# Attention front of a two-layer network: another order of the groups, modulation rows moved to the router, first loads in order of need

## The chip, the core and the metric

The kernel runs on one core of a Trainium2 chip. The metric is the device time of one execution in microseconds (us). A core has five engines that run side by side, each with its own instruction stream: TensorE (PE; PEld is its weight load), VectorE (DVE), ScalarE (ACT), GpSimd (POOL) and SyncE (SP), which here only issues DMA transfers. They wait for each other through semaphores.

## The reference, cut to what matters

Two layers; each is modulated attention, then a modulated mixture of experts. The change touches layer 0's attention and the router behind it.

```python
mod = (_silu(L0_c) @ L0_wmod).reshape(..., 6, 1, -1)      # rows sa, ca, ga, sb, cb, gb of 256
ga = (2 * (ga >= 0) - 1) * jnp.maximum(jnp.abs(ga), 0.25) # gb alike
h = _layernorm(x) * (1 + ca) + sa                          # x: 2048 x 256
q = (h @ Wq).reshape(.., 16, 16); k = h @ Wk; v = h @ Wv   # 16 heads, one key and value head of 16
scores = where(causal, q k / 4, -inf); out = softmax(scores) @ v
x = x + ga * (out @ Wo + bo)
h = _layernorm(x) * (1 + cb) + sb
x = x + gb * moe0(h)                                       # router: top 1 of 8, capacity 320
mod = (_silu(L1_c) @ L1_wmod)...                           # the same six rows for layer 1
```

## The kernel before

**Chunks, groups, units.** `phase_front` computes layer 0's attention. The 2048 queries are four chunks of 512 (`c`), the 16 heads four groups of 4 (`g`), so there are 16 groups `(c, g)`. A group of chunk `c` has `4(c+1)` units, one for each tile of 128 keys; in its last four, the diagonal units, only 4, 3, 2, 1 of the four query tiles are computed and POOL masks the diagonal block (L841). There are 160 units, numbered 0 to 159 in the order in which the groups run. A unit is 16 score matmuls in each of two halves (L424, four share the array at a time), two exponentials on ACT (L581, one for each half) and the value matmuls of the unit before (L440). So the two exponentials of unit n are number 2n+1 and 2n+2 of 320, and the first marks its start.

**Products for the maxima.** The softmax subtracts each row's maximum, so each group needs a first pass ahead of it: for 16 tiles of queries and each chunk of keys up to its own, four matmuls (L367) write a product to one of three PSUM banks (`f_r`, the ring), and DVE reduces it: 128x512 plainly (L641), the diagonal ones of 128, 256, 384 or 512 columns together with a causal mask (L638 and a read of its result). Below these are the full and the diagonal products. A group has 16, 32, 48 or 64 of them by chunk, 640 in all. When a group's last one is reduced, DVE makes its row of maxima (L645 to L649, `k_m2t`), SP writes it into the queries' tile (L749, 8 DMAs a group), and the group's first unit waits for it.

**The order of the work** is a table made by `front_schedule`. 45 products go in between the projections of chunks 2 and 3 (`EARLY`, `PRE`); the others are spread evenly over the units so that a group's last one comes 4 units (`MARGIN`) before its first unit, a unit taking at most 5 (`issued[u] = max(issued[u], issued[u + 1] - 5)`); what does not fit goes into unit 0. The ring also carries the rows of the modulation (M, L352: two fp32 matmuls, ACT copies them out, L534) and the output steps A, B, C of each tile of 128 tokens (A: turn the values, DVE divides, L390, L654, L655; B: turn back, ACT copies, L398, L538; C: output projection, DVE adds it to x and takes the statistics, L407, L661, L90). PE, DVE and ACT each take the entries in this one order.

**Queries through DRAM.** The projections make q and k as three bfloat16 parts (L328, L335, L529). SP writes the parts of a chunk to DRAM (L730) and reads them back in another layout (L740); a group's first product waits for that load (`q_in`). For chunk 0 the heads 4 to 15 have a load of their own (`q_rest`).

**Ahead and behind.** Before the projections DVE normalises x in four quarters (L78 to L83, L605), ACT issues the four loads of x, SP all others. Behind the front comes `phase_router` (layernorm, 8 logits, top 1, rank within the expert, then 16 scatters by POOL, L1274, `slots_ready` sets them free), then the experts. A phase starts when the one before has ended on all engines.

## Time and profile before

| | us |
|---|---|
| median of 3 runs | 1171.91 (1171.73 to 1172.45) |
| the profiled execution | 1172.97 |
| its span in the trace | 1171.3 |
| PE, DVE, ACT, POOL busy over the span | 84%, 54%, 46%, 25% |
| unit 0 starts, unit 159's exponentials end | 83.45, 517.3 |
| first router instruction | 529.9 |

The profile's page gives the busy time of each engine and, in 40 slices of 29.3 us, its busy tenths. PEclk is the clock that TensorE was granted, 1.00 being 2.4 GHz and 0.50 being 1.2 GHz. A row of windows gives each engine's busy time and its number of instructions (x) in a stretch; a row of the timeline gives the start, the length, engine, line, what was written from what, and in brackets how long the engine had been idle and what ended that.

### The profile page before, as it was taken

Reading aid. Unit: us, or ns where it says so; the run is one execution under the profiler, and the core shown is the slowest. Engines: PE = TensorE matmul, PEld = TensorE weight load, DVE = VectorE, ACT = ScalarE, POOL = GpSimd, SP = SyncE. Lnnn points to the kernel's source line nnn. Section 1 sums busy time; section 2 is a strip of 40 time slices with the busy share of each in tenths; the row PEclk is TensorE's granted clock in tenths of the full one; section 3 lists DMA queues with packets and bytes.
Section 4 is the critical chain, followed back from the end, with each engine's and each line's share of the span. In section 5 each row is a group of like instructions: output and inputs, shape, how many; then the busy total and the mean of one; then the engine's idle time right before and its main releaser. Section 6 shows DMA issues by size and latency. Waiting matters only on the chain. (4 is left out here: it accounts for less than half of the span.)

```text
span 1171.3 us, 25113 instructions
## 1 busy us (share of the span) xinstructions
PE 985.8 (84%) x9938; PEld 639.1 (55%) x9943; DVE 629.3 (54%) x1719; ACT 535.6 (46%) x834; POOL 297.4 (25%) x344
## 2 busy tenths in 40 slices
PE   4888999999999999985079999649557599999994
PEld 2434444344334544332057777537335599999993
DVE  4256889999999999345100000185676633333331
ACT  1543665666666777764023222155045443333330
POOL 3001431101001100110502222235720035455442
PEclk9988999999999999998579999969789799999997
DMA  6682000100003000008314555210045722322333
GB/s 205 165 156 41 3 2 3 69 28 2 3 3 3 3 2 3 1 1 292 119 28 115 168 115 168 37 54 1 1 162 186 235 41 47 49 45 49 48 47 90
DMA packets 73406, 81.66 MB, mean 70 GB/s; under 512 B 23121, under 2 KB 64465, under 8 KB 72609
## 3 DMA queue, kind: packets, MB, share of 16 engines
q1 hardware_dynamic: 58912, 61.18, 18.7%
q0 software_dynamic: 12288, 17.10, 8.7%
q10 hardware_dynamic: 2112, 2.10, 0.6%
q8 instruction: 64, 1.05, 0.4%
q14 instruction: 30, 0.24, 0.1%
HBM read 58.19 MB, written 24.13 MB: 70 GB/s over the span
## 5 line engine op out<-in xcount | busy, mean ns | idle before, releaser
L581 ACT ACTIVATE k_prob<-f_s 128x1024 f32<-128x1024 f32 (+3 forms) x320 | 270.1, 896 | 123.2 <-PE f_s L424 122.2
L641 DVE TENSOR_REDUCE k_mpart<-f_r 128x1 f32<-128x512 f32 x384 | 250.0, 684 | 12.4 <-PE f_r L367 10.3
L367 PE MATMUL f_r<-k_ks,k_qs 112*32 112x512 bf16 (+3 forms) x2560 | 213.2, 354 | 11.8 <-DVE k_mpart L641 6.6
L424 PE MATMUL f_s<-k_qs,k_ks 114*32 114x512 bf16 (+3 forms) x2560 | 176.6, 351 | 6.4 <-DMA k_qs<-k_m2t 4.2
L440 PE MATMUL f_o<-k_prob,k_vaug 128*32 128x512 f32 (+3 forms) x1280 | 150.4, 532 | 0.5 <-POOL k_prob L841 0.3
L841 POOL TENSOR_SCALAR_AFFINE_SELECT k_prob<-k_prob 128x256 f32<-128x256 f32 x128 | 51.4, 406 | 384.5 <-ACT k_prob L581 383.2
L367 PEld LDWEIGHTS f_r<-k_ks,k_qs 112*32 112x32 bf16 x2560 | 70.8, 95 | 138.3 <-DVE k_mpart L641 64.8
L638 DVE CUSTOM_DVE_ANT_0 k_unread<-f_r,k_causal 128x128 bf16<-128x128 f32 (+3 forms) x256 | 120.6, 484 | 31.6 <-PE f_r L367 30.7
L424 PEld LDWEIGHTS f_s<-k_qs,k_ks 114*32 114x32 bf16 x2560 | 65.5, 97 | 75.0 <-issue 21.4
L1975 DVE TENSOR_TENSOR mid<-silu_g,e_u 128x512 f32<-128x512 f32 x39 | 26.8, 688 | 126.7 <-PE e_u L1880 126.7
L1415 DVE SCALAR_TENSOR_TENSOR outr<-p_o,rows,k_mod 128x256 f32<-128x256 f32 x16 | 7.7, 484 | 141.3 <-PE p_o L1372 141.3
L1880 PEld LDWEIGHTS e_g<-xT,wg 128*128 128x128 f32 x624 | 76.9, 195 | 3.3 <-ACT xT L1935 1.4
L1880 PE MATMUL e_g<-xT,wg 128*128 128x128 f32 x624 | 77.5, 278 | 0.9 <-ACT xT L1935 0.9
L1361 PE MATMUL p_h<-rowsT,k_wi 128*128 128x320 f32 x256 | 73.3, 446 | 4.9 <-issue 3.8
L1880 PE MATMUL e_u<-xT,wu 128*128 128x128 f32 x624 | 76.4, 276 | 0.0
L2023 POOL DMA_INDIRECT xb<-h_rows,k_tok_of x39 | 45.0, 1155 | 121.3 <-PE e_x L1874 66.1
L2032 POOL DMA_INDIRECT sum<-y,k_row_of x39 | 62.0, 1591 | 53.0 <-DVE y L1986 50.2
L1401 ACT ACTIVATE mid<-p_h 128x320 f32<-128x320 f32 x64 | 28.0, 437 | 103.2 <-PE p_h L1361 103.2
L1891 PE MATMUL e_y<-k_w1T,mid 128*128 x312 | 73.6, 379 | 0.0
L1880 PEld LDWEIGHTS e_u<-xT,wu 128*128 128x128 f32 x624 | 73.2, 193 | 0.0
L1361 PEld LDWEIGHTS p_h<-rowsT,k_wi 128*128 128x128 f32 x256 | 49.4, 195 | 26.6 <-issue 8.2
L1891 PEld LDWEIGHTS e_y<-k_w1T,mid 128*128 128x128 f32 x312 | 56.3, 190 | 6.1
(299 smaller groups left out, 1280.3 us busy)
## 6 DMA issues: line engine op xcount, KB each, us to landing
r_raw<-in_L_ffn_w_dram SPq DMA_DIRECT2D x24, 512.0 KB, 5.8
k_wi<-in_L_ffn_wi_dram SPq DMA_DIRECT2D x8, 1024.0 KB, 5.1
k_wo_e<-in_L_ffn_wo_dram SPq DMA_DIRECT2D x8, 1024.0 KB, 7.7
k_qs<-q_dram SPq DMA_DIRECT2D x6, 768.0 KB, 9.6
sum<-k_x SPq DMA_DIRECT2D x8, 512.0 KB, 7.0
q_dram<-k_q_parts SPq DMA_DIRECT2D x12, 256.0 KB, 6.4
disp<-k_wmod SPq DMA_DIRECT2D x2, 1310.0 KB, 7.2
rows<-disp SPq DMA_DIRECT2D x8, 262.0 KB, 2.7
```

What stands on the lines that cost most here:

```text
L367: last = nc.tensor.matmul(dst[32 * j:32 * (j + 1), :], qs[0:KROWS, c, GH * g + hs, q0:q0 + 32], ks[0:KROWS, QC * ck:QC * ck + w], start=Tr ...
L424: last = nc.tensor.matmul(sc[h % 2][32 * j:32 * (j + 1), i, off:QC], ks[0:KALL, k0:k0 + 32], qs[0:KALL, c, GH * g + 2 * pair + i, off:QC], ...
L440: last = nc.tensor.matmul(ot[32 * j:32 * (j + 1), off:QC], vaug[:, kt, :], prob[:, u % 2, j, off:QC], start=(kt == 0), stop=(kt == TQ * (c ...
L581: nc.scalar.activation(prob[:, u % 2, 2 * pair:2 * pair + 2, off:QC], sc[h % 2][:, :, off:QC], ACT.Exp, scale=HD ** -0.5).then_inc(e_done, 1)
L638: nc.vector.tensor_tensor_reduce(unread[:, r % RING, 0:w], bank(r)[:, 0:w], causal[:, QC - w:QC], 1.0, NEG, ALU.add, ALU.max, mpart[:, s % ...
L641: nc.vector.reduce_max(mpart[:, s % 2, hs, t, ck:ck + 1], bank(r)[:, 0:w], AX.X).then_inc(ring_used[r % RING], 1)
L841: nc.gpsimd.affine_select(out=block_, in_=block_, compare_op=ALU.is_ge, fill=0.0, base=0, pattern=[[0, 2], [1, P]], channel_multiplier=-1) ...
L1361: last = nc.tensor.matmul(ph[n % 2][:, :], wi[:, s, t, P * n:P * (n + 1)], rowsT[:, s, t, :], start=(t == 0), stop=(t == KH - 1))
L1880: last = nc.tensor.matmul(out[:, P * c:P * (c + 1)], w[:, s, F1 * t + P * c:F1 * t + P * (c + 1)], xT[:, s, t, :], start=(t == 0), stop=(t ...
L1891: last = nc.tensor.matmul(py[s][:, :], m[:, s, P * c:P * (c + 1)], k.w1T[:, e, 2, D * c:D * (c + 1)], start=(c == 0), stop=(c == FT - 1))
L2023: nc.gpsimd.indirect_dma_start(out=xb[:, s, :], out_offset=None, in_=k.h_rows, in_offset=bass.IndirectOffsetOnAxis(ap=k.tok_of[:, b:b + 1] ...
L2032: nc.gpsimd.indirect_dma_start(out=k.sum1, out_offset=bass.IndirectOffsetOnAxis(ap=k.row_of[:, b:b + 1], axis=0), in_=y[:, s, :], in_offse ...
```

## The change

It has four parts. (1) `ORDER`: the groups run as (0,0), (1,0), (2,0), (3,0), then (3,1) to (3,3), (2,1) to (2,3), (1,1) to (1,3), (0,1) to (0,3). The 45 early products are then 16 of chunk 0 and 29 of chunk 1. The output steps of a chunk follow its last group, so those of chunk 0 come last. All four chunks' outputs need a place (`oT`, `kept`), and POOL's steps (gate, bias, clearing, `rstd2`) are put at other units. (2) The ring keeps only the modulation rows GA, SB, CB, GB of layer 0. The unused rows SA and CA are dropped; the six of layer 1 are computed in layer 0's router from a load of their own, with 6 fp32 matmuls of 512 columns, 3 copies and 5 DVE instructions. (3) The first loads go out in the order in which they are used; three quarters of x move from ACT's to SP's queue. (4) The row of maxima takes 4 DMAs a group, each of two rows, for 8.

```diff
-MOD_ORDER = [GA, SA, CA, SB, CB, GB] + list(range(MODS, 2 * MODS))
+MOD_ORDER = [GA, SB, CB, GB]
-ORDER = [(c, g) for c in range(NC) for g in range(NG)]
+ORDER = ([(c, 0) for c in range(NC)] + [(NC - 1, g) for g in range(1, NG)]
+         + [(c, g) for c in range(NC - 2, -1, -1) for g in range(1, NG)])
...
-            first = (start[4] + 2, start[8] + 2, start[15] - 4, NU)[c]
+            first = min(start[s] + TQ * (c + 1) + 2, NU - len(order) + 1) if c else NU
...
-    NROWDMA = 8
+    NROWDMA = 4
...
-        oT = sb("oT", [P, 2, NG, QC])
+        own = sb("oT", [P, 2, NG, QC])
+        oT = [own[:, 0], own[:, 1], kept[:, 0], kept[:, 1]]
...
-            for c in range(NC):
-                act.dma_start(quarter(k.x, c), xv[:, TQ * c:TQ * (c + 1), :]).then_inc(x_in[c], 16)
+            act.dma_start(quarter(k.x, 0), xv[:, 0:TQ, :]).then_inc(x_in[0], 16)
...
                 if u == NU - 6:
-                    scale_row(0, CB)
-                    gate_row(0, GB)
-                if u == NU - 4:
-                    for m in (CA, CB):
-                        scale_row(1, m)
-                    for m in (GA, GB):
-                        gate_row(1, m)
+                    scale_row(CB)
+                    gate_row(GB)
...
                 for b in range(4):
-                    for part in range(2):
-                        dst = qs[BROW + part:BROW + part + 1, c, GH * g:GH * (g + 1), :]\
-                            .rearrange("o h (t b r) -> o (h t) b r", b=4, r=32)[:, :, b, :]
-                        sp.dma_start(dst, m2t[32 * b + NT * part:32 * b + NT * (part + 1), s, :]).then_inc(rows_in[s], 16)
+                    dst = qs[BROW:BROW + 2, c, GH * g:GH * (g + 1), :].rearrange("o h (t b r) -> o (h t) b r", b=4, r=32)[:, :, b, :]
+                    sp.dma_start(dst, m2t[32 * b:32 * (b + 1), s, :]).then_inc(rows_in[s], 16)
...
-                if u == 16:
+                if u == 12:
                     fold_gate()
-                if u in (17, 18, 19, 24):
-                    add_bias((17, 18, 19, 24).index(u))
-                if u == 26:
+                if u in range(13, 17):
+                    add_bias(u - 13)
+                if u == 24:
                     clear()
...
             if layer == 0:
+                sp.dma_start(wmod[:, :, :], a.L1_wmod.rearrange("(t p) n -> p t n", p=P)).then_inc(wmod_in, 16)
                 xv = k.sum0[0:T, :].rearrange("(i p) d -> p i d", p=P)
...
+            if layer == 0:
+                pe.wait_ge(wmod_in, 16)
+                pe.wait_ge(hT_ready, 2 * NC)
+                for n in range(3):
+                    for t in range(KH):
+                        last = nc.tensor.matmul(tp[n // 2][n % 2][:, :], k.mod[:, 1, GB, P * t:P * (t + 1)], wmod[:, t, QC * n:QC * (n + 1)],
+                                                start=(t == 0), stop=(t == KH - 1))
+                    last.then_inc(rows_done, 1)
+
             pe.wait_ge(chosen_ready, 1)
...
                 nc.vector.tensor_copy(scat[:, 0, :], small[3][:, :]).then_inc(slots_ready, 1)
+                dve.wait_ge(mod_ready, 3)
+                m = k.mod[:, 1, :, :].rearrange("p (b m) d -> p b m d", b=2)
...
```

**The first loads, on SP.** `k_x` is x, `k_wq`, `k_wk`, `k_wv` are the projections' weights, `k_wmod` the modulation's. Before:

```order
L714 DMA k_c_col<-in_L_c_dram 128x2x1 x2
L717 DMA k_wmod<-in_L_wmod_dram 128x2x512
L719 DMA k_wq<-in_L_attn_Wq_dram 128x2x256
L719 DMA k_wk<-in_L_attn_Wk_dram 128x2x16
L719 DMA k_wv<-in_L_attn_Wv_dram 128x2x16
L720 DMA k_kpart<-in_kpart_dram 128x4
L721 DMA k_bo<-in_L_attn_bo_dram 128x256
L722 DMA k_wo<-in_L_attn_Wo_dram 128x2x256
L724 DMA k_wmod<-in_L_wmod_dram 128x2x1024
L725 DMA k_wmod<-in_L_wmod_dram 128x2x1536
```

And of the change:

```order
L711 DMA k_wmod<-in_L_wmod_dram 128x2x512
L713 DMA k_wq<-in_L_attn_Wq_dram 128x2x256
L713 DMA k_wk<-in_L_attn_Wk_dram 128x2x16
L713 DMA k_wv<-in_L_attn_Wv_dram 128x2x16
L714 DMA k_kpart<-in_kpart_dram 128x4
L715 DMA k_bo<-in_L_attn_bo_dram 128x256
L717 DMA k_x<-in_L_attn_x_dram 128x4x256 x3
L718 DMA k_wmod<-in_L_wmod_dram 128x2x1024
L719 DMA k_wo<-in_L_attn_Wo_dram 128x2x256
```

The quarters 1 to 3 of x now stand behind the weights in the same queue, and layer 1's modulation weights (128x2x1536) are no longer loaded here.

**The last products between the projections of chunk 2, on PE.** L335 takes a part away, L343 is the values' projection of chunk 2, L328 the first projection of chunk 3. Before:

```order
L335 MATMUL f_o<-k_ks,k_minus 128x512
L367 MATMUL f_r<-k_ks,k_qs 32x128 x4
L367 MATMUL f_r<-k_ks,k_qs 32x256 x4
L343 MATMUL f_r<-k_wv,k_h 128x16 x8
L328 MATMUL f_s<-k_h,k_wq_by_d 128x512 x2
```

And of the change:

```order
L339 MATMUL f_o<-k_ks,k_minus 128x512
L370 MATMUL f_r<-k_ks,k_qs 32x512 x4
L370 MATMUL f_r<-k_ks,k_qs 32x128 x4
L347 MATMUL f_r<-k_wv,k_h 128x16 x8
L332 MATMUL f_s<-k_h,k_wq_by_d 128x512 x2
```

The two products were of group (0,1) and are now of (1,0), whose queries are chunk 1's.

**The first units, on PE.** L424 (L427) are scores, L440 (L443) values, L352 (L355) a modulation row. Before, from unit 0 into unit 2:

```order
L424 MATMUL f_s<-k_qs,k_ks 32x512 x16
L424 MATMUL f_s<-k_qs,k_ks 32x384 x8
L367 MATMUL f_r<-k_ks,k_qs 32x256 x4
L424 MATMUL f_s<-k_qs,k_ks 32x384 x8
L440 MATMUL f_o<-k_prob,k_vaug 32x512 x4
L352 MATMUL f_r<-k_wmod,k_silu_c 128x256 x2
L424 MATMUL f_s<-k_qs,k_ks 32x256 x8
```

And of the change, the whole of unit 0 and the start of unit 1:

```order
L427 MATMUL f_s<-k_qs,k_ks 32x512 x8
L370 MATMUL f_r<-k_ks,k_qs 32x384 x4
L427 MATMUL f_s<-k_qs,k_ks 32x512 x8
L370 MATMUL f_r<-k_ks,k_qs 32x512 x16
L370 MATMUL f_r<-k_ks,k_qs 32x128 x4
L370 MATMUL f_r<-k_ks,k_qs 32x512 x8
L370 MATMUL f_r<-k_ks,k_qs 32x256 x4
L370 MATMUL f_r<-k_ks,k_qs 32x512 x8
L370 MATMUL f_r<-k_ks,k_qs 32x384 x4
L370 MATMUL f_r<-k_ks,k_qs 32x512 x20
L370 MATMUL f_r<-k_ks,k_qs 32x128 x4
L370 MATMUL f_r<-k_ks,k_qs 32x512 x8
```

Unit 0 had no product and has 20 now.

## Rows read from the trace of the kernel before

**Rows 1.** The page's 40 slices: busy tenths of PE, and TensorE's clock.
```profile
PE   4888999999999999985079999649557599999994
...
PEclk9988999999999999998579999969789799999997
```

In rows 2 each row is: stretch, its length, busy us (x instructions) of PE, PEld, DVE, ACT, POOL, then PEclk, the share of the DMA engines and GB/s.

**Rows 2.** Windows cut where units 0, 4, 8, 12, 28, 44, 68, 76, 92, 140, 144, 152, 156 start.
```profile
83.40:99.85 16.45, 11.99 (x153) 5.23 (x148) 5.70 (x26) 6.35 (x11) 3.21 (x8) 0.83 0.68 114
99.85:115.40 15.55, 15.10 (x196) 7.57 (x190) 11.19 (x41) 7.25 (x13) 3.20 (x8) 0.85 0.02 3
115.40:129.95 14.55, 13.67 (x200) 6.88 (x196) 11.86 (x35) 7.09 (x13) 3.20 (x8) 1.00 0.01 1
129.95:173.70 43.75, 42.93 (x684) 19.99 (x680) 39.02 (x115) 29.04 (x41) 20.11 (x24) 1.00 0.02 3
173.70:220.60 46.90, 43.56 (x716) 18.35 (x708) 45.07 (x126) 27.04 (x34) 7.44 (x17) 1.00 0.02 3
220.60:287.95 67.35, 65.83 (x1007) 29.27 (x1001) 62.47 (x159) 43.76 (x54) 7.42 (x17) 1.00 0.11 42
287.95:306.95 19.00, 18.64 (x328) 7.88 (x324) 18.26 (x48) 13.34 (x17) 3.21 (x8) 1.00 0.02 3
306.95:352.75 45.80, 43.89 (x712) 16.87 (x705) 44.99 (x106) 29.04 (x33) 3.23 (x8) 1.00 0.01 3
352.75:472.40 119.65, 118.40 (x1924) 55.77 (x1920) 113.94 (x254) 86.69 (x99) 9.61 (x24) 1.00 0.11 3
472.40:481.85 9.45, 7.96 (x114) 3.43 (x110) 3.11 (x12) 5.49 (x9) 3.20 (x8) 1.00 0.02 3
481.85:502.90 21.05, 20.58 (x222) 7.98 (x218) 3.74 (x10) 16.70 (x20) 0.00 (x0) 1.00 0.01 2
502.90:510.95 8.05, 7.48 (x100) 2.13 (x96) 5.99 (x21) 7.54 (x8) 1.01 (x1) 1.00 0.00 1
510.95:517.45 6.50, 5.66 (x96) 1.89 (x88) 0.00 (x0) 5.21 (x8) 3.23 (x8) 1.00 0.01 3
```

**Rows 3.** The start, DVE's first instruction and the first loads' times to landing.
```profile
13.02 0.29 DVE L677 COPY k_wk_rep<-k_wk 128x256 f32<-128x256 f32 x1 [13.02 <-DMA k_wv<-in_L_attn_Wv_dram]
...
k_x<-in_L_attn_x_dram ACTq DMA_DIRECT2D x4, 512.0 KB, 7.6
k_wmod<-in_L_wmod_dram SPq DMA_DIRECT2D x1, 1536.0 KB, 12.8
```

**Rows 4.** Window in the start (columns as in rows 2; the last is GB/s).
```profile
6.00:8.00 2.00, 0.00 (x0) 0.00 (x0) 0.00 (x0) 0.59 (x1) 0.00 (x0) 1.00 1.07 379
```

**Rows 5.** Source line L740, 50 to 52 us: the load of chunk 1's queries.
```profile
L740 SPq DMA_DIRECT2D k_qs<-q_dram x3: 319/422/423, 50.6 to 51.4; - x3
...
DMA to landing us min/median/max: 7.6/11.4/13.2
```

**Rows 6.** Timeline: chunk 2's values' projection, diagonal and full reductions, an output's addition.
```profile
60.72 1.96 PE L343 MATMUL f_r<-k_wv,k_h 128*128 128x16 f32 x16 [0.32 <-DVE k_mpart L638]
...
71.28 0.29 DVE L638 CUSTOM_DVE_ANT_0 k_unread<-f_r,k_causal 128x128 bf16<-128x128 f32 x1 [0.94 <-PE f_r L367]
...
72.93 0.29 DVE L638 CUSTOM_DVE_ANT_0 k_unread<-f_r,k_causal 128x128 bf16<-128x128 f32 x1
...
470.03 1.94 DVE L641 TENSOR_REDUCE k_mpart<-f_r 128x1 f32<-128x512 f32 x3
...
522.14 0.42 DVE L661 TENSOR_TENSOR k_x<-k_x,f_r 128x256 f32<-128x256 f32 x1 [0.46 <-PE f_r L407]
```

**Rows 7.** Timeline: PE at unit 4.
```profile
98.76 1.04 PE L424 MATMUL f_s<-k_qs,k_ks 114*32 114x512 bf16 x8 [2.85 <-DMA k_qs<-k_m2t]
```

**Rows 8.** Timeline: two fp32 matmuls of 512 columns; in the router the ranks, the first scatter.
```profile
27.35 1.88 PE L328 MATMUL f_o<-k_h,k_wk_rep 128*128 128x512 f32 x4
...
557.06 0.29 PE L1052 MATMUL r_prank<-r_chosen_bf,k_before 128*128 128x128 bf16 x1 [4.72 <-DVE r_chosen_bf L1143]
...
564.28 1.23 POOL L1274 DMA_INDIRECT disp<-r_hx,r_scat  x1 [33.67 <-DVE r_scat L1177]
```

More of the change, by code:

```diff
@@ L274, in phase_front @@
         ZW = E * CAP // P * DW // 2
-        zeros = wmod[:, 1, :, :].rearrange("p t n -> p (t n)")[:, 0:ZW]
+        zeros = room[:, 0:ZW]
         marks = sb("marks", [P, 3, E * CAP // P], U32)
         x_in = [sem(f"f_x_in{c}") for c in range(NC)]
-        c_in, wmod_in = sem("f_c_in"), [sem(f"f_wmod_in{n}") for n in range(3)]
+        c_in, wmod_in = sem("f_c_in"), [sem(f"f_wmod_in{n}") for n in range(2)]
         wq_in, const_in, wo_in = sem("f_wq_in"), sem("f_const_in"), sem("f_wo_in")
@@ L450, in _ @@
                         last = nc.tensor.matmul(ot[:, 2 * m + half:2 * m + half + 1],
-                                                wmod[:, 0, t, D * m + P * half:D * m + P * (half + 1)],
-                                                silu_c[:, 0, t, 0:1], start=(t == 0), stop=(t == KH - 1))
+                                                wmod[:, t, D * m + P * half:D * m + P * (half + 1)],
+                                                silu_c[:, t, 0:1], start=(t == 0), stop=(t == KH - 1))
             last.then_inc(col_done, 1)
@@ L625, in gate_row, with scale_row @@
                 step(nc.vector.scalar_tensor_tensor(gate, gate_sgn[:, :], -1.0, gate_mag[:, :], ALU.add, ALU.mult))
-            def scale_row(layer, m):
-                have(layer, m)
-                step(nc.vector.tensor_scalar_add(k.mod[:, layer, m, :], k.mod[:, layer, m, :], 1.0))
+            def scale_row(m):
+                have(m)
+                step(nc.vector.tensor_scalar_add(k.mod[:, 0, m, :], k.mod[:, 0, m, :], 1.0))
             def maxima(r, n):
@@ L721, in _ @@
             sp.dma_start(bo[:, :], a.L0_attn_bo.partition_broadcast(P)).then_inc(const_in, 16)
+            for c in range(1, NC):
+                sp.dma_start(quarter(k.x, c), xv[:, TQ * c:TQ * (c + 1), :]).then_inc(x_in[c], 16)
+            sp.dma_start(wmod[:, :, 2 * D:MODS * D], wm[:, :, 2 * D:MODS * D]).then_inc(wmod_in[1], 16)
             sp.dma_start(wo[:, :, :], a.L0_attn_Wo.rearrange("(t p) n -> p t n", p=P)).then_inc(wo_in, 16)
-            sp.dma_start(wmod[:, 0, :, 512:MODS * D], wm[0][:, :, 512:MODS * D]).then_inc(wmod_in[1], 16)
-            sp.dma_start(wmod[:, 1, :, :], wm[1]).then_inc(wmod_in[2], 16)
             def spill(c):
@@ L808, in clear @@
             def clear():
-                pool.wait_ge(ring_done, at[("M", MOD_ORDER[-1])] + 1)
+                for part in range(3):
+                    pool.wait_ge(spilled[part], 16 * NC)
                 nc.gpsimd.memset(zeros[:, :], 0.0).then_inc(zero_set, 1)
@@ L842, in _ @@
                                                 pattern=[[0, 2], [1, P]], channel_multiplier=-1).then_inc(masked, 1)
-            ln_rstd(nc, pool, k, NC - 1, var2_ready, rstd2_ready)
+            for n in range(len(rstd_after), NC):
+                rstd2(n)
             pool.wait_ge(rstd2_ready, NC)
@@ L1106, in _ @@
                 nc.scalar.activation(ex[j][:, :, :], tmp[j][:, :, :], ACT.Exp).then_inc(exp_done, 1)
+            if layer == 0:
+                for n in range(3):
+                    act.wait_ge(rows_done, n + 1)
+                    nc.scalar.copy(k.mod[:, 1, 2 * n:2 * n + 2, :].rearrange("p m d -> p (m d)"),
+                                   tp[n // 2][n % 2][:, :]).then_inc(mod_ready, 1)
             if layer == 1:
```

70 lines of the change are left out of this document (41 added, 29 removed).

## The prediction

> **What bounds the kernel now.** I read the page's slices first [rows 1]. TensorE is busy in nine tenths or more of nearly every slice from 120 to 470 us and its clock stands at 2.4 GHz there; the front is the longest piece, and the change touches it and the router only. So the question is what a unit costs, and I cut the front where its units start [rows 2]. The reader is to see three regimes.
> - In the 48 units 92 to 139 the windows hold 119.65 us, 2.49 us a unit, with PE busy for 118.40 and DVE for 113.94. Four products a unit load both engines fully.
> - In units 28 to 43 (five products each) DVE is busy 45.07 of 46.90 us and PE 43.56: DVE ends last, 2.93 a unit.
> - Units 152 to 155 have no product and take 8.05 us, 2.01 each, with ACT busy 7.54 and DVE waiting or on small rows. The exponentials end last there.
>
> So a product near the end is nearly missing work, and at the start it is dear. Units 0 to 11 are worse than any: 46.55 us for 12 small diagonal units [rows 2], PE busy 11.99 of the first 16.45. Unit 4's scores waited 2.85 us for the row of maxima [rows 7]. SP had issued it behind the loads of chunk 3's queries. The clock is 0.83 and 0.85 in the first two rows, and eleven modulation rows go through the ring here.
>
> **The units, part by part.** The order tables of both kernels were laid beside each other, unit by unit. 104 of the new kernel's units have the same shape, the same products and the same output steps as units of the old one, only elsewhere: its 4 to 19 are the old 76 to 91 (45.80 us), 20 to 67 the old 92 to 139 (119.65), 84 to 107 the old 44 to 67 (67.35), 120 to 135 the old 12 to 27 (43.75); one modulation row moves between them. I price them at what they took, 276.55 together [rows 2], and no gain or loss is in them. The other 56 old units took the rest of 434.05 us: 46.55 (0 to 11), 46.90 (28 to 43), 19.00 (68 to 75), and 9.45 + 21.05 + 8.05 + 6.50 = 45.05 (140 to 159), together 157.5. The 56 new ones hold the same 163 products, in other company:
> - Units 0 to 3 have 35 products, 20 of them in unit 0. DVE: 23 full ones at 1.94/3 = 0.647, 12 diagonal ones at (72.93 - 71.28)/4 = 0.41 [rows 6], 0.8 for a row of maxima: 20.6. PE needs less. I take 23, because I expect some low clock behind unit 0. Ends 20.6 and 30.
> - 68 to 83: three products. A full unit sheds one (512 columns at 2.4 GHz, 0.21) and comes from 2.49 to about 2.29, the four diagonal ones 7.0 in all: 34.5. Ends: 31 (as with no product, 2.01) and 40 (as with four).
> - 108 to 119: 2.67 products: 24, ends 22 and 29.
> - 136 to 143: two small products, two output steps C, and POOL's `rstd2` ahead of a mask at unit 138: 17, ends 14.5 and 20.
> - 144 to 151: eight diagonal units with four small products each. DVE 16 x 0.41 + 0.8 per four, with the output steps: 16, ends 14 and 18.
> - 152 to 159: eight diagonal units with no product and eight output steps. Units 156 to 159 took 6.50 with none and 140 to 143 9.45 with four and a wait of about 1.3 for their row of maxima [rows 2]: 2 x 8.1 = 16.2. Ends 13 and 20.
>
> Sum 130.7, so the units give back 157.5 - 130.7 = 26.8 us. Eight modulation rows fewer on the ring are a part of it, the rest is waiting that is now filled. The row of maxima with 4 DMAs instead of 8 is priced at nothing: four units pass between its last product and its use, and where they are full units that covers it.
>
> The burst in unit 0 is the place where another rule speaks. The trace has TensorE pausing for DVE again and again through units 28 to 43, 3.34 us in 46.90, at a clock of 1.00; it has the clock at 0.83 where PE was busy 11.99 of 16.45 [rows 2]. The Trainium skill, page "TensorE: Matmul & The Clock Gate", section "A second HAM failure mode: psum-queue depth-cycling", says that matmuls which cycle through PSUM banks with small pauses can make the clock swing between its two levels. By that rule the heavy units would not hold 2.4 GHz and the sum would be the last rival's below; the trace agrees for long pauses and not for short ones.
>
> **The start.** DVE's first instruction waits for the values' weights until 13.02 [rows 3]; everything up to unit 0 follows from there. They share the DMA engines with four quarters of x (512 KB each) and two larger loads of modulation weights, of which the first steps need one quarter only. What they need is 512 (x) + 512 (modulation) + 256 (query weights) + 32 KB = 1.31 MB. At 340 to 379 GB/s, the rate of the windows at 6 us [rows 4], that is 3.6 us of transfer; it starts near 3.4 and small rows come last, so I take 8.3 us, a gain of 4.7 (ends 3.5 and 6). The second quarter of x, 0.5 MB more, is there about 1 us later, before DVE has done the first.
>
> **A wait that is added.** The last two products between chunk 2's projections are now of group (1,0) and wait for chunk 1's queries. That load is issued until 51.4 and its last part lands 13.2 later, at 64.6 [rows 5]. PE reaches this place at 60.3, just before the values' projection at 60.72 [rows 6]. Both shift with the start, so PE stands 4.3 us, and behind it stand the values' projection and all of chunk 3's. Ends: 0 (if the load is quicker with less traffic) and 5. This eats the gain of the start.
>
> **Chunk 3's projections.** 27 products are reduced between them, now half of them full: 0.24 more for each of 9 in the stretch where DVE sets the pace, less a row of maxima (0.8) that moves into unit 0: + 1.5. Ends 0 and 3.
>
> **The tail.** One more output step C stands behind unit 159. It runs while ACT copies the last values; its DVE work (0.42 for the addition [rows 6], as much for the statistics) delays the first division a little: + 0.7. Ends 0 and 1.5.
>
> **The router.** PE ends its logits 4.72 us before it gets the chosen experts at 557.06 [rows 8]. Two fp32 matmuls of 512 columns take 1.88 [rows 8], so the six new ones take 5.6, 0.9 too long; DVE, which needs the ranks, has steps of its own for most of that: + 0.5 (ends 0 and 2). DVE's five instructions stand behind the slots, beside the scatters that begin at 564.28 [rows 8]. Layer 1's load of 1536 KB goes ahead of the copies of x and of the experts' weights; at the rate of the start it takes 4.2 us of the DMA engines, which were quiet before the scatter. I price it at nothing; if it delays the scatter, 4.
>
> **Sum.** - 26.8 - 4.7 + 4.3 + 1.5 + 0.7 + 0.5 = - 24.5 against the profiled execution's 1172.97: 1148.5. That execution lies 1.06 above the median of 1171.91, so the median to expect is **1147.4**. Its own range, the ends not all on one side at once: 1140 to 1155.
>
> **Rivals.**
> - *The wait isn't there.* Less traffic ahead of the queries, 0 instead of 4.3: 1143. For it: 2.5 MB fewer in the first 20 us. Against: those had landed by 20.3 (7.5 + 12.8 [rows 3]), 30 us before the load in question.
> - *A unit with fewer products costs no less.* If units 68 to 83, 108 to 119 and 136 to 143 cost what units with four products cost, 40 + 29 + 18.5 instead of 75.5: + 12, 1159. For it: no unit of before has three. Against: units 152 to 155 at 2.01.
> - *Small diagonal units are slow in themselves.* 12 new units of chunk 0 stand at the end. At the 46.55 of units 0 to 11 instead of about 24.4: + 22, 1170. For it: the chain of exponential, mask and values is the same. Against: units 156 to 159 take 6.50 for four, and unit 4 was held by a DMA [rows 7].
> - *Slower: the clock.* Unit 0 leaves PE idle for more than half of some 12 us. If the clock then stays at 1.2 GHz while PE feeds DVE, a unit of five products needs 2 x (2.49 + 0.21) us of PE where DVE needs 2.93, 2.5 more each. Over units 1 to 16 that is 40: 1187. It decides from about 10 units on. Against: in the second row of [rows 2] PE was busy 15.10 of 15.55, and the clock was back at 1.00 afterwards.
> - That the change doesn't do what it says is excluded by its order table.
>
> **Chances.** Forecast 0.62, no wait 0.12, fewer products no cheaper 0.13, diagonal units slow 0.07, clock 0.06. The range for 8 in 10 goes from 1138 (no wait, and some ends low) to 1161. A change under 0.2% (2.3 us) can't be told from none: faster 0.92, within 0.03, slower 0.05.
>
> **What the profile after would show.** DVE's first instruction near 8.3; PE idle some 4 us before the values' projection of chunk 2, released by a DMA; unit 0 starting at 83.45 - 4.7 + 4.3 + 1.5 = 84.6 and lasting some 12 us with DVE full; units 20 to 67 in 119.7 us; unit 159 done near 492; the router some 24 us earlier and of equal length. The prediction is wrong if the clock stays at 0.5 beyond unit 4, if the same-shaped stretches take other times, or if the last twelve units need more than 3 us each.

## The result: less than half of the forecast gain

The changed kernel took 1162.09 us (median of 6, 1161.18 to 1164.53) beside 1172.24 for the kernel before on the same chip: ratio 0.9909, interval 0.9893 to 0.9925. It is faster, but the forecast was 1147.4 with a range from 1138 to 1161, so the time lies outside. Between the profiled executions the gain is 1172.97 - 1162.2 = 10.8 us where 24.5 were forecast; 13.7 are missing. The kernel before took 1170.79 to 1173.49 us (medians) in the sessions of the experiments, so kernels of different sessions are compared by their ratios and not by their medians.

The page's slices of the kernel after, which answer to [rows 1] (busy tenths of PE, and TensorE's granted clock):

```profile
PE   5889899999999999957099999558657599999994
...
PEclk9987999999999999998599999769788799999998
```

The front is still the longest piece, and from 145 to 493 us PE is busy for nine tenths or more of every slice. The windows cut at the new kernel's units show more. They answer to [rows 2]: length, then busy us of PE, PEld, DVE, ACT, POOL, then PEclk, DMA share and GB/s. The rows are, in order, chunk 3's projections, then units 0 to 3, 4 to 19, 20 to 67, 68 to 83, 108 to 119, 120 to 135, 136 to 143, 144 to 151 and 152 to 159.

```profile
61.70:87.20 25.50, 23.24 (x173) 11.36 (x175) 15.27 (x45) 7.12 (x10) 0.00 (x0) 0.83 0.61 122
...
87.20:112.85 25.65, 23.52 (x249) 8.69 (x244) 20.06 (x51) 6.45 (x11) 3.21 (x8) 0.67 0.32 57
...
112.85:161.35 48.50, 44.95 (x716) 17.43 (x712) 46.38 (x109) 29.89 (x35) 14.69 (x15) 1.00 0.01 2
161.35:280.05 118.70, 117.47 (x1928) 54.07 (x1924) 113.93 (x254) 86.68 (x99) 11.84 (x25) 1.00 0.01 3
280.05:315.05 35.00, 34.87 (x583) 14.97 (x578) 28.52 (x71) 28.84 (x33) 3.21 (x8) 1.00 0.01 3
...
381.30:405.95 24.65, 24.52 (x424) 10.51 (x420) 18.42 (x55) 21.05 (x25) 3.21 (x8) 1.00 0.01 3
405.95:448.95 43.00, 42.17 (x680) 19.43 (x676) 39.17 (x117) 28.18 (x38) 6.41 (x16) 1.00 0.01 3
448.95:467.55 18.60, 16.75 (x268) 7.42 (x264) 10.50 (x48) 13.36 (x17) 4.08 (x9) 1.00 0.56 4
467.55:486.40 18.85, 17.02 (x338) 8.24 (x338) 16.17 (x75) 11.14 (x18) 6.41 (x16) 1.00 0.02 4
486.40:503.55 17.15, 15.89 (x219) 7.17 (x211) 5.91 (x18) 12.11 (x21) 6.41 (x16) 1.00 0.01 3
```

Against the forecast, stretch by stretch (us):

| stretch | forecast | measured | difference |
|---|---|---|---|
| start of unit 0 | 84.6 | 87.25 | + 2.65 |
| units 0 to 3 | 23 | 25.65 | + 2.65 |
| units 4 to 19 | 45.80 | 48.50 | + 2.70 |
| units 20 to 67 | 119.65 | 118.70 | - 0.95 |
| units 68 to 135 | 169.6 | 168.9 | - 0.7 |
| units 136 to 143 | 17 | 18.60 | + 1.60 |
| units 144 to 151 | 16 | 18.85 | + 2.85 |
| units 152 to 159 | 16.2 | 17.15 | + 0.95 |
| first expert's first product less the end of the units | 78.45 | 78.05 | - 0.4 |
| from there to the end | 576.6 | 578.8 | + 2.2 |

Lines 5 and 9 are worked out: 34.5 + 67.35 + 24 + 43.75 against 448.95 - 280.05; 594.71 - 517.45 + 1.2 against 581.60 - 503.55. The end of the units is the end of the last value matmul here (503.55), and 517.45 lies in the last value matmuls, which end at 517.68. The table of times ahead of the prediction has 517.3 for the end of unit 159's exponentials; in the trace the last one ends at 516.73. The units took 416.35 us where 407.25 were forecast and 434.05 were taken before.

The timeline of the kernel after on DVE and PE, answering to [rows 3] and [rows 6] (start, us, engine, line, operation, and in brackets the idle time before and what ended it):

```profile
8.53 0.29 DVE L675 COPY k_wk_rep<-k_wk 128x256 f32<-128x256 f32 x1 [8.53 <-DMA k_wv<-in_L_attn_Wv_dram]
...
11.95 1.40 DVE L78 BATCH_NORM_STATS2 k_stats<-k_x 128x6 f32<-128x256 f32 x4 [1.20 <-DMA k_x<-in_L_attn_x_dram]
```

```profile
61.07 0.73 PE L370 MATMUL f_r<-k_ks,k_qs 112*32 112x512 bf16 x8 [4.54 <-DMA k_qs<-q_dram]
61.73 3.60 PE L347 MATMUL f_r<-k_wv,k_h 128*128 128x16 f32 x16
...
457.89 0.64 PE L443 MATMUL f_o<-k_prob,k_vaug 128*32 128x256 f32 x8 [1.22 <-POOL k_prob L841]
```

The first row is the forecast gain of the start (8.3 was said). The second is a wait that was said not to be: the second quarter of x isn't there in time. The third is the added wait, 4.54 us for 4.3. Right behind it the values' projection takes 3.60 us where it took 1.96 before [rows 6]: the granted clock stands at 0.5 from 59.9 to 70.2 us, and again from 87.2 to 104.3. In the kernel before it was at 0.5 for 3.4 us four times and for 6.8 once in the whole front.

### The profile page after: what moved, and what is told of

The parts are those of the page before. It is cut to its first block and busy times, and to the rows that moved or that the text cites. A ratio compares the mean times of both kernels' runs of the same rounds, so it can differ in the third digit from the quotient of the medians.

```text
span 1160.4 us, 24988 instructions
## 1 busy us (share of the span) xinstructions
PE 980.0 (84%) x9918; PEld 635.9 (55%) x9923; DVE 632.0 (54%) x1714; ACT 534.2 (46%) x830; POOL 297.8 (26%) x344
## 5 line engine op out<-in xcount | busy, mean ns | idle before, releaser
L370 PE MATMUL f_r<-k_ks,k_qs 112*32 112x512 bf16 (+3 forms) x2560 | 212.0, 359 | 16.2 <-DVE k_mpart L639 7.3
L427 PE MATMUL f_s<-k_qs,k_ks 114*32 114x512 bf16 (+3 forms) x2560 | 173.9, 350 | 1.9 <-ACT k_prob L579 1.3
L443 PE MATMUL f_o<-k_prob,k_vaug 128*32 128x512 f32 (+3 forms) x1280 | 146.5, 531 | 1.5 <-POOL k_prob L841 1.4
L427 PEld LDWEIGHTS f_s<-k_qs,k_ks 114*32 114x32 bf16 x2560 | 64.2, 97 | 79.3 <-issue 27.8
L2002 DVE TENSOR_TENSOR mid<-silu_g,e_u 128x512 f32<-128x512 f32 x39 | 26.8, 688 | 124.7 <-PE e_u L1907 124.7
L2050 POOL DMA_INDIRECT xb<-h_rows,k_tok_of x39 | 45.3, 1161 | 121.5 <-PE e_x L1901 64.5
```

Source lines behind the costliest of these rows:

```text
L370: last = nc.tensor.matmul(dst[32 * j:32 * (j + 1), :], qs[0:KROWS, c, GH * g + hs, q0:q0 + 32], ks[0:KROWS, QC * ck:QC * ck + w], start=Tr ...
L427: last = nc.tensor.matmul(sc[h % 2][32 * j:32 * (j + 1), i, off:QC], ks[0:KALL, k0:k0 + 32], qs[0:KALL, c, GH * g + 2 * pair + i, off:QC], ...
L443: last = nc.tensor.matmul(ot[32 * j:32 * (j + 1), off:QC], vaug[:, kt, :], prob[:, u % 2, j, off:QC], start=(kt == 0), stop=(kt == TQ * (c ...
L2050: nc.gpsimd.indirect_dma_start(out=xb[:, s, :], out_offset=None, in_=k.h_rows, in_offset=bass.IndirectOffsetOnAxis(ap=k.tok_of[:, b:b + 1] ...
```

## The experiments

Each was timed in several executions beside the kernel before, except one that ran once. Ratios are to the kernel before, with their interval.

**The change without its order.**

```diff
-ORDER = ([(c, 0) for c in range(NC)] + [(NC - 1, g) for g in range(1, NG)] + ...)
+ORDER = [(c, g) for c in range(NC) for g in range(NG)]
```

> Everything of the change but the order of groups: the groups run in the old order (and the output steps start at their old units), first loads, router rows and the four row DMAs stay new. Theory A (the new order pays about 11 us: units 0 to 159 went from 434.05 to 416.3 us, of which some 3 are the eight modulation rows that left the ring, and it costs the 4.54 us wait for chunk 1's queries): this kernel keeps the start (PE's first turn 3.3 us early), has no such wait, and keeps the 2 us lost behind the router: about 1169 us, units 0 to 159 in some 431 us. Theory B (the order pays little, the start and the router's rows carry the change): 1164 us or less, and the units in under 427. In both, if the 0.24 us that PE loses between two experts comes from the code around it and not from the order, it is here too.

1163.71 us, 0.9922 (0.9900 to 0.9945). That overlaps the change's interval: the new order, on which nearly the whole forecast rested, is worth about nothing in this kernel. Its windows (units 0 to 3, 4 to 11, 12 to 19, 20 to 159):

```profile
80.10:93.40 13.30, 11.90 (x156) 5.09 (x152) 5.71 (x27) 6.34 (x12) 3.20 (x8) 0.85 0.76 140
93.40:116.90 23.50, 19.72 (x360) 9.03 (x356) 21.41 (x71) 11.93 (x20) 7.89 (x19) 1.00 0.01 2
116.90:138.45 21.55, 18.81 (x336) 9.03 (x332) 19.42 (x59) 14.00 (x18) 13.04 (x13) 1.00 0.01 3
138.45:503.60 365.15, 354.12 (x5516) 154.78 (x5512) 315.04 (x781) 249.61 (x303) 43.77 (x100) 1.00 0.05 10
```

All 160 units take 423.5 us: 10.55 of the 17.7 us that the units gained come with the old order kept. Units 0 to 11 lost 9.75 of their 46.55 [rows 2]. Of the 10.55, 1.0 is no part of the change: units 100 to 103 took 11.11 us in the profiled execution of the kernel before and 10.07 to 10.10 in the next experiment's kernel and here, because PE's value matmuls paused once in unit 100. Its cause stayed open. The order brings the other 7.15, and it costs as much ahead of them: unit 0 starts at 80.1 here and at 87.25 in the change. Theory B came true, with 1163.71 for "1164 or less" and 423.5 for "under 427".

**One part alone in the kernel before: rows of maxima with 4 DMAs.**

```diff
-                    for part in range(2):
-                        dst = qs[BROW + part:BROW + part + 1, ...]
-                        sp.dma_start(dst, m2t[32 * b + NT * part:32 * b + NT * (part + 1), s, :])
+                    dst = qs[BROW:BROW + 2, ...]
+                    sp.dma_start(dst, m2t[32 * b:32 * (b + 1), s, :])
```

> The kernel before with one part of the change alone: a row of maxima is brought back with 4 DMAs instead of 8. Theory A (PE's wait of 2.85 us at unit 4 and that of some 1.4 us at unit 140 are the 8 DMAs' issuing and landing): the two waits shrink to under 0.5 us each, units 4 to 7 take 12.5 to 13.5 instead of 15.55, units 140 to 143 take 8.1 instead of 9.46; the kernel about 1169 us. Theory B (the row waits behind the loads of chunk 3's queries, and the old output steps hold units 140 to 143): both waits stay over half their length, 1171 to 1173 us.

1169.21 us, 0.9977 (0.9963 to 0.9992). Windows of units 0 to 3, 4 to 7 and 140 to 143:

```profile
85.70:99.35 13.65, 12.46 (x153) 5.36 (x149) 5.69 (x26) 6.35 (x11) 3.22 (x8) 0.81 0.54 98
99.35:113.00 13.65, 12.96 (x196) 6.75 (x192) 11.16 (x41) 7.21 (x13) 3.22 (x8) 1.00 0.02 3
468.90:476.95 8.05, 7.89 (x118) 3.47 (x112) 2.92 (x12) 5.49 (x10) 3.22 (x8) 1.00 0.02 3
```

They took 16.45, 15.55 and 9.45 [rows 2], and unit 4's scores wait no longer [rows 7]. Theory A for the waits: both were the 8 DMAs. The wait of 2.85 us ended at 98.76, before unit 4's first exponential at 99.85, so it is units 0 to 3 that are 2.8 shorter; with the 1.4 of units 140 to 143 the DMAs cost 4.2. The 1.9 of units 4 to 7, where the theory looked for the wait, go with TensorE's clock, which was 0.85 there and is 1.00. The median moved by 2.0 only, and in the profiled execution unit 0 started 2.3 us later than before.

**The change without its second part: the second layer's rows back in the front.**

```diff
-MOD_ORDER = [GA, SB, CB, GB]
+MOD_ORDER = [GA, SA, CA, SB, CB, GB] + list(range(MODS, 2 * MODS))
```

> The whole change but its second part: the second layer's modulation rows and the two rows that moved with them stay in the front (twelve rows less two, in units 1 to 12), its weights are loaded behind the first loads; order, first loads and 4 DMAs are new. Theory A (the eight rows cost the old front some 8 of the 10.4 us that the change gained there with the old order kept, because each holds PE for 1.13 us at the place where DVE and PE are both full): here they cost as much, units 0 to 19 take 80 us or more instead of 74.1, the router and the experts give 1.5 to 2 us back: about 1167 to 1169 us. Theory B (in the new order PE waits for DVE in units 0 to 19, so the rows hide): units 0 to 19 under 76 us, and the kernel 1161 to 1163 us. The 0.24 us lost between two experts should be gone if it comes with the router's rows.

1166.32 us, 0.9958 (0.9942 to 0.9975). Windows of units 0 to 3, 4 to 11 and 12 to 19, and the first expert's first product:

```profile
86.60:112.20 25.60, 23.47 (x248) 8.65 (x244) 20.06 (x51) 6.44 (x11) 3.21 (x8) 0.67 0.32 57
112.20:143.50 31.30, 29.45 (x392) 13.87 (x388) 24.99 (x60) 16.34 (x26) 5.37 (x12) 1.00 0.01 2
143.50:167.30 23.80, 23.36 (x364) 9.44 (x360) 22.42 (x49) 16.36 (x18) 6.92 (x3) 1.00 0.01 1
```

```profile
587.47 3.03 PE L1369 MATMUL p_h<-rowsT,k_wi 128*128 128x320 f32 x5 [1.03 <-ACT rowsT L1406]
```

Units 0 to 19 take 80.7 us, 6.55 more than the change's 74.15: 0.82 us for each of eight rows (POOL's bias additions also stand at their old units here). That price isn't the same everywhere: with the old order the units of the two kernels with 4 DMAs, rows in the front and rows in the router, differ by 3.1 us in all. The expectation says twelve rows less two; the kernel has all twelve. Behind the units the router with its rows costs nothing: from unit 159's exponential to the first expert 78.7 us before, 78.7 in the kernel with the old order and router rows, 80.1 here without router rows and 80.3 in the change. The 1.5 us come with the order (one more output step behind the units), not with the rows. The table shows less of it because it counts from the last value matmul, and in the new order that one stands behind an output step.

**Gate row, bias and modulation rows later.**

```diff
-GATE_AT = 8
+GATE_AT = 72
-        extras[1 + n].append(("M", m))
+        extras[67 + n].append(("M", m))
-                if u == 12:            # fold_gate
+                if u == 74:
-                if u in range(13, 17): # add_bias
+                if u in range(75, 79):
```

> Gate row, folding of the gate and the bias additions move from units 8 to 16 to units 72 to 78, where DVE has three products a unit, and the four modulation rows from units 1 to 4 to 67 to 70. Theory A (units 4 to 19 took 48.47 us and not the 45.80 of the same units of before because the four gate instructions of DVE, 1.53 us, and POOL's bias additions stand in units that DVE bounds): units 4 to 19 come back to 45.8 to 46.3, units 68 to 83 stay within 0.5 us of 35.0, units 0 to 3 lose the modulation rows' 0.5 us or so; the kernel takes 1158.5 to 1160 us. Theory B (units 4 to 19 are slow because DVE starts them late behind the burst of unit 0): they stay within 0.7 us of 48.47 and the kernel takes 1161.5 to 1162.5 us.

1163.16 us, 0.9915 (0.9892 to 0.9937): no gain. Windows of units 0 to 3, 4 to 19, 20 to 67 and 68 to 83:

```profile
87.40:109.80 22.40, 20.29 (x236) 6.72 (x232) 19.31 (x51) 5.50 (x8) 3.25 (x8) 0.62 0.36 64
109.80:155.65 45.85, 43.54 (x712) 16.70 (x708) 45.14 (x106) 29.52 (x34) 3.23 (x8) 1.00 0.01 2
155.65:275.65 120.00, 118.78 (x1932) 58.32 (x1928) 114.88 (x259) 87.06 (x100) 11.84 (x25) 1.00 0.01 3
275.65:314.90 39.25, 38.13 (x596) 18.09 (x592) 29.18 (x70) 29.99 (x36) 14.76 (x15) 1.00 0.01 3
```

Here the two forecasts that failed come true: 22.40 for 23, and 45.85 for 45.80. So the 5.3 us missing in units 0 to 19 are the four modulation rows and the gate's work, which the comparison of shapes had left out. Units 0 to 3 lost 3.25 us, where 0.5 had been expected of their rows. Half of theory A fell, though: units 68 to 83 did not hide it, they took 4.25 more and units 20 to 67 1.3 more. There PE is full (34.87 of 35.00), and a row or a step that leaves DVE's tight place enters PE's.

**Six products ahead instead of five.**

```diff
-        issued[u] = max(issued[u], issued[u + 1] - 5)
+        issued[u] = max(issued[u], issued[u + 1] - 6)
```

> Of the plan one number: a unit may hold 6 products ahead of its need instead of 5, so that unit 0 has 9 products and not 20, and units 1 to 7 have 6 each; the 19 units of the front take the same products. Theory A (units 0 to 3 and the begin of unit 4 were slow because PE paused for DVE through the burst in unit 0 and the clock stood at 0.5 from 87.2 to 104.3 us): with fewer products at one place the clock stays at 1.00 for most of it, units 0 to 19 take 70 to 72 us together instead of 74.1, the kernel 1158 to 1160 us. Theory B (DVE does the same products in the same time, wherever they stand, and the clock falls for the same pauses, only spread): units 0 to 19 within 1 us of 74.1, the kernel 1161.5 to 1163 us.

1161.28 us, 0.9913 (0.9895 to 0.9931). Units 0 to 19:

```profile
86.60:160.50 73.90, 66.46 (x956) 25.60 (x952) 66.23 (x159) 36.37 (x46) 17.96 (x23) 0.93 0.11 21
```

Theory B: 73.9 us for 74.15, although the clock stood at 0.5 for 10 us in three pieces and not for 17. That doesn't show that the low clock is free, because the products stand elsewhere too, and PE was busy as long as DVE (66.46 and 66.23). A cleaner pair is the change and the kernel with fewer narrow products below, which has the same instructions up to unit 135. Its clock came back at 101.3 us and not at 104.3; its units 0 to 3:

```profile
87.50:111.55 24.05, 21.93 (x248) 8.38 (x244) 20.05 (x51) 6.35 (x12) 3.20 (x8) 0.72 0.34 60
```

That is 1.6 us less than the change's 25.65. Unit 0, the burst, took 12.5 and 12.7 us, at the low clock in both; unit 1 took 4.28 and 5.75, and its value matmuls 1.03 and 1.93. So in the burst the low clock cost nothing that these traces show, and in unit 1 it cost 1.5 us.

**No product between chunk 2's last step and chunk 3's projections.**

```diff
-EARLY = {2: (2,) * 9, 3: (3,) * 9}
+EARLY = {2: (2,) * 8 + (0,), 3: (0, 0, 0, 5, 5, 5, 5, 5, 4)}
```

> The last product between chunk 2's projections and all between chunk 3's three projections are moved behind these, so that PE has 6 fp32 products of chunk 3 to do while chunk 1's queries land; the number of early products stays 45. Theory A (the wait of 4.54 us costs its length, and 1.3 more because the clock stands at 0.5 from 59.9 to 70.2 us behind it): the wait is gone, the clock stays at 1.00 there, unit 0 starts 4 to 6 us earlier (81 to 83 instead of 87.25) and the kernel takes 1156.5 to 1158 us. Theory B (DVE sets the pace between chunk 3's projections, 27 products, and they can't start before the queries are there): the wait only moves, unit 0 starts less than 2 us earlier and the kernel takes 1160.5 or more.

1157.97 us, 0.9870 (0.9839 to 0.9901), from executions in two groups, three at 1155.0 and three at 1160.9 to 1163.3. The profiled one is of the upper group. Its window from the values' projection to unit 0:

```profile
61.30:85.40 24.10, 21.80 (x161) 9.18 (x163) 14.86 (x44) 7.03 (x11) 0.00 (x0) 0.79 0.82 161
```

The wait is gone, but the clock fell at 75.4 for 27.3 us, and unit 0 started only 1.85 us earlier, at 85.4. Neither theory is settled by it; the next one was made for that.

**Chunk 1's queries in two loads.**

```diff
-                load_queries(c, 0, H, q_in[c])
+                load_queries(c, 0, GH if c == 1 else H, q_in[c])
+                if c == 1:
+                    load_queries(c, GH, H, q_rest[1])
```

> Of the load of chunk 1's queries the first four heads (a quarter of its 768 KB) are brought in first with a semaphore of their own, as chunk 0's are; the products of (1,0) need no more. Nothing else is moved. Theory A (PE's 4.54 us wait before chunk 2's values is the landing of 768 KB, and the low clock from 59.9 to 70.2 us follows from it): the wait falls to under 1 us, unit 0 starts 4 to 6 us earlier (81.5 to 83), the kernel 1156 to 1158.5 us. Theory B (the load is late by its issue and its way, not by its size): the wait stays over 3 us, 1161 to 1162.5 us. Theory C (the wait goes, but the clock falls later in the front all the same): unit 0 at 82 to 84, the kernel 1158.5 to 1160.5 us.

1155.04 us, 0.9862 (0.9837 to 0.9887). PE at the place of the wait, and the window from there to unit 0:

```profile
58.48 0.46 PE L370 MATMUL f_r<-k_ks,k_qs 112*32 112x512 bf16 x8
59.26 1.96 PE L347 MATMUL f_r<-k_wv,k_h 128*128 128x16 f32 x16 [0.33 <-DVE k_mpart L636]
```

```profile
59.30:82.95 23.65, 21.97 (x170) 9.63 (x174) 15.88 (x49) 7.19 (x11) 0.00 (x0) 0.90 0.72 147
```

Theory A: the wait was the landing of 768 KB of which 192 were needed. No wait is left, and the values take 1.96 us again. Unit 0 starts 4.3 us earlier, at 82.95: PE had no wait of 4.54 and took 1.8 less from the values to unit 0, but reached this place 2.0 later than in the change (its clock had stood at 0.5 for 6.8 us before, and for 3.4 there). By the ratios the kernel gains 5.5 us, and the two intervals leave 2 to 9, so the median can't tell the gain from the wait's length. With this the order is worth something: 0.9862 against 0.9922 with the old order, which has no such wait (its last products between chunk 2's projections are of chunk 0): 7 us.

**The second quarter of x first.**

```diff
+            sp.dma_start(quarter(k.x, 1), xv[:, TQ:2 * TQ, :]).then_inc(x_in[1], 16)
             sp.dma_start(kpart[:, :], a.kpart).then_inc(const_in, 16)
```

> One load is moved: the second quarter of x goes ahead of the constants and the bias (behind the values' weights) on SP's queue. Theory A (DVE waits 1.20 us for it before its second statistics, and PE's first turn hangs on that): the wait shrinks to 0 to 0.5, PE's first turn starts about 1 us earlier than 15.41, and all of that reaches the end: about 1161.1 us. Theory B (the DMA engines are full there, so that an earlier quarter holds up the first quarter and the weights by as much, or ACT and POOL wait for the constants instead): first turn within 0.3 us, 1162 us.

1161.93 us, 0.9905 (0.9882 to 0.9928). DVE's second statistics:

```profile
10.50 1.40 DVE L78 BATCH_NORM_STATS2 k_stats<-k_x 128x6 f32<-128x256 f32 x4
```

They start at 10.50 without a wait and PE's first turn at 14.06 instead of 15.41. Unit 0 gains 0.8, because the wait for the queries grew to 4.93. Theory A for the place; at the end it can't be told from nothing.

**Two groups of chunk 1 at the begin.**

```diff
+ORDER = ([(0, 0), (1, 0), (1, 1), (2, 0)] + [(NC - 1, g) for g in range(NG)]
+         + [(c, g) for c in range(NC - 2, -1, -1) for g in range(1 + (c == 1), NG)])
```

> The order begins with two groups of chunk 1 ((0,0), (1,0), (1,1), (2,0), (3,0)), the rest as in the change; unit 0 has 13 products and the next ones 5, and 8 units fewer stand at the end. Theory A (the lump of products that the new order owes before unit 12 is what makes the begin dear): units 0 to 11 and what they hold come cheaper by 3 us or more, the last 24 units the same, the kernel 1158 to 1160 us. Theory B (what is missing at the begin comes back at the end and the other way round, since PE and DVE are both near full over the whole front): 1161 to 1163.5 us. The wait for chunk 1's queries (4.54 us) is in this one too.

1155.87 us, 0.9869 (0.9847 to 0.9891), better than either theory. Units 0 to 11, 12 to 19 and 20 to 67:

```profile
86.65:131.30 44.65, 39.93 (x572) 16.61 (x568) 38.33 (x107) 20.20 (x30) 8.04 (x19) 0.89 0.19 34
131.30:154.20 22.90, 20.99 (x360) 8.05 (x352) 22.48 (x55) 13.54 (x17) 14.82 (x14) 1.00 0.01 3
154.20:276.30 122.10, 119.89 (x1960) 56.09 (x1956) 117.83 (x264) 87.16 (x100) 10.26 (x25) 1.00 0.01 2
```

Units 0 to 11 take 44.65 us instead of 51.15, with 8 products fewer and DVE busy for 38.33 us instead of 43.74; units 20 to 67 give 3.4 us back, and units 136 to 159 take 3.1 more, where theory A had them unchanged. All units together: 3.6 less. The profiled execution is 6.3 shorter; 2.3 of that lie behind the first expert, where the code is the same.

**Fewer narrow products at the end (run once).** Three of four heads' maxima of the last three groups are left out, so those groups' values are others.

```diff
-        rows = [(hs, qt) for hs in range(GH) for ...]
+        rows = [(hs, qt) for hs in range(GH - 1 if s > 12 else 0, GH) for ...]
```

> The change, with 36 of the 48 narrow products and reductions of the last three groups left out (three of four heads' maxima; the output is not the reference's in those groups). It prices them where units 136 to 151 took 37.46 us and 33 were forecast. Theory A (PE ends last there: a narrow product holds PE for 0.22 to 0.38 us whatever DVE does, beside scores, values and output steps that take 28 us): the sixteen units take 28 to 31 us. Theory B (output steps, POOL's masks and the exponentials set the time, the products hide beside them as in the forecast): they still take 34 us or more.

Units 136 to 143 and 144 to 151:

```profile
447.60:465.45 17.85, 15.28 (x220) 6.07 (x212) 5.50 (x25) 13.30 (x17) 4.08 (x9) 1.00 0.67 4
465.45:480.30 14.85, 13.76 (x238) 6.14 (x242) 6.26 (x27) 11.17 (x20) 6.40 (x16) 1.00 0.02 3
```

32.7 us for 37.45, between the theories: 24 narrow products fewer save 4.0 us in the second stretch (0.17 each), 12 fewer only 0.75 in the first. So the first is held by something else. With one execution there is no interval here.

**POOL's root behind the units.** The root of chunk 2's variances leaves the place ahead of unit 138's masks.

```diff
-            rstd_after = {... if at[("C", TQ * c + TQ - 1)] in unit_of}
+            rstd_after = {... if at[("C", TQ * c + TQ - 1)] in unit_of
+                          and unit_of[at[("C", TQ * c + TQ - 1)]] + 1 not in diags}
```

> The change with one POOL instruction moved: the root of chunk 2's variances no longer stands ahead of unit 138's masks but behind the last unit. Theory A (it waits 2.16 us for DVE and runs 1.01 in front of the masks, and PE's 1.22 us wait for a mask at 457.89 is its doing): the wait is gone, units 136 to 143 take 17.2 to 17.6 us instead of 18.63, the kernel about 1161 us. Theory B (the mask only ends last by a little, the exponentials or DVE's reductions are as late): the units stay over 18.2 us, 1162 us. The rest of the 5.3 us by which units 136 to 159 missed the forecast is then the narrow products and output steps of PE.

1160.73 us, 0.9886 (0.9868 to 0.9905). Units 136 to 143:

```profile
448.90:466.20 17.30, 16.67 (x268) 7.50 (x264) 10.56 (x48) 13.39 (x18) 3.22 (x8) 1.00 0.77 4
```

Theory A: 17.3 for 18.6, and 17 had been forecast. PE's wait of 1.22 us for a mask is gone.

**Together.** Two groups of chunk 1 first, queries in two loads, the quarter of x early; then the same with a second group of chunk 2; then the first with POOL's root moved.

> The change with two groups of chunk 1 at the begin, chunk 1's queries in two loads, and the second quarter of x ahead of the constants. If these three gains are of different waits they add up: unit 0 starts at 80 to 82, the kernel 1150 to 1152 us (1155.9 less 4 to 5 for the queries' wait, less 0.8 for the quarter). If the begin of the units waits for something else once unit 0 comes earlier (rows of maxima, DVE's load of products), 1153 to 1155.5 us.

> As the one before, and in addition a second group of chunk 2 ahead of chunk 3, so that the products due before (3,0) spread over 44 units and not 32; later groups of chunk 2 move 12 units out of the stretch that needs 2.67 products a unit. Theory A (a product in a unit with five costs 0.44 us and one in a unit with three 0.30, from 2.93, 2.49 and 2.19 us a unit): some 12 products move from the one to the other, 1 to 2 us faster than the one before. Theory B (PE and DVE are both near full there, a product costs the same everywhere): within 1 us of it.

> The best kernel so far (two groups of chunk 1 at the begin, split load of chunk 1's queries, second quarter of x early) and the same move of POOL's root, which stands ahead of unit 146's masks there. Units 144 to 151 took 21.23 us there; if the mask ends last they come to 19.8 to 20.3 and the kernel to 1147 to 1148 us; if not, the kernel stays within 0.5 us of 1148.65.

1148.65 us, 0.9825 (0.9797 to 0.9853); 1150.80, 0.9830 (0.9808 to 0.9851); 1150.73, 0.9801 (0.9783 to 0.9819). The three can't be told apart, and each beats the change. The first came out below both of its forecasts, and its unit 0 started at 79.24 where 80 to 82 was said. By the ratios the gains add up: 0.40, 0.47 and 0.04 in a hundred make 0.9818 of the change's 0.9909, and 0.9825 was measured. A second group of chunk 2 changes the units by 0.7 us (theory B), and POOL's root changes nothing here: units 144 to 151 take 21.2 us in both (PE doesn't wait for a mask there). The last kernel's median lies 2.1 above 1148.65 and not within 0.5, with 1173.49 for the kernel before in its session and 1170.79 in the other's.

## Why the prediction failed, step by step

The largest part is the price of the new units: they gave back 17.7 us where 26.8 were forecast. That is 9.15 of the missing 13.7; 2.65 lie ahead of unit 0, 2.2 behind the first expert.

- **What bounds the front**: right. Where DVE or PE is full, the same shapes took the same time to 0.8% (units 20 to 67), and the 0.95 us between them are the one pause of unit 100 before.
- **"104 units have the same shape; no gain or loss is in them"**: failed for units 4 to 19. Products and output steps are the same, but one modulation row, DVE's four gate instructions and POOL's bias additions stand there that didn't stand in old units 76 to 91. The later gate row gave 45.85 for 45.80 and so named the 2.7 us.
- **Units 0 to 3 at 23**: the sum over DVE was 20.6 and left the rows out; without them 22.40 was measured. "PE needs less" failed: PE was busy for 23.52 of the 25.65 us and DVE waited 5.0 us for it. The low clock, for which 2.4 us had been put in, is a part of that: 1.6 us less were measured where it ended 3 us earlier.
- **"136 to 151 at 17 + 16"**: the terms were mis-sized. In the first, POOL's root had been seen, its price of 1.3 us had not. In the second, DVE's own work (16.17) was right, but PE had 17.02 and had not been summed: a narrow product costs both engines. With 24 of them gone DVE was busy for 6.26 us and PE for 13.76 of 14.85. That the rest of the 18.85 is the two engines waiting for each other is argued, not shown. Units 152 to 159 missed by 0.95, where eight output steps stand in units without products.
- **"The other units give back 26.8"**: they gave 17.7. What it was made of was wrong as well: 10.55 came with the old order kept, 7.15 from the order. Of the 10.55, the two waits for rows of maxima made 4.2, though the 4 DMAs were priced at nothing because "four units pass" (small units before unit 4 did not cover it), and 1.0 was the pause of unit 100. The rest is the eight rows, less what the gate's earlier work costs, and clock; the runs don't split it further.
- **The start, - 4.7**: 4.5 for DVE, as said; "the second quarter of x is there ... before DVE has done the first" failed by 1.20 us. PE's first turn came 3.3 us earlier.
- **The added wait, + 4.3**: 4.54. But its price was not its length. The clock stood at 0.5 for 10.2 us from within the wait on, while PE had fp32 products for chunk 3, so the stretch from chunk 2's values to unit 0 grew by 2.8 us and not by the 1.5 of "chunk 3's projections" (whose own terms, 9 times 0.24 less 0.8, give 1.4). Without the wait that stretch took 23.7 us and not 25.5. With the order, unit 0 starts 7.15 us later than without it, which is all that the order gains in the units; 4.3 of that went with the wait.
- **Tail + 0.7, router + 0.5**: 0.8 together instead of 1.2 as the table counts, 1.5 from unit 159's exponential; the router's part is zero.
- **Behind the first expert, 0**: 2.2 us more, from 576.6 to 578.8. It can't be laid on the change: the same stretch took 575.9 in the kernel with rows in front, 576.5 with two groups of chunk 1 first, and 578.3 in the kernel before with 4 DMAs, whose code there is the old one. Executions of the same code differ by as much, and the cause stayed open.

```profile
581.60 2.49 PE L1388 MATMUL p_h<-rowsT,k_wi 128*128 128x320 f32 x4 [1.03 <-ACT rowsT L1425]
```

This is the row of the kernel after from which its 578.8 us run to the end of the span at 1160.4.

Of the rivals, the dear small units (1170) and the slow clock (1187) came in pieces: units 136 to 159 took 5.4 us more than forecast, and the clock did stand at 0.5 from 87.2 to 104.3, through the burst of unit 0, and then was at 1.00 from 104.3 us to the end of the units. The Trainium skill, page "TensorE: Matmul & The Clock Gate", section "A second HAM failure mode: psum-queue depth-cycling", says that small pauses between groups of matmuls can make the clock swing. The trace agrees that it swung: it fell at 87.2, behind pauses of 0.2 to 0.5 us for DVE, and was back at 104.3. It agrees on lost throughput for unit 1 (the 1.5 us above) and doesn't show any for unit 0.

## What to carry to other kernels

Before a stretch is priced by one of the same shape, list every instruction in it, the side work of all engines too; what stands in a full stretch costs its length wherever it is moved. A wait on the engine that sets the pace costs its length and can cost more behind it, where the clock has fallen (here 1.8 us behind 4.54); splitting the load so that what is needed first lands alone took it away. A transfer priced at nothing because full units cover it has to be looked at where the units are small. A change of several parts should be priced part against part: here the part that looked small (8 rows and 4 DMAs) brought more than the order, whose gain in the units was lost ahead of them.
